# Identity products on TensorE ahead of the first transposes, and one value unit moved ahead of the first local softmax

## The reference

```python
x = x + local_attention(layernorm(x))              # 8 heads, chunks of 12 queries over 24 keys,
                                                   # relative positions, tanh cap 50, softmax, Wpost
x = x + cross_attention(layernorm(x), ctx_1024)    # 16 heads of 64, 512 context rows, rope on keys,
                                                   # clipped logits, softmax, Wo
x = x + mixture_ffn(layernorm(x))                  # 12 experts, top 3 routing, 128 -> 512 -> 128
```

## Time and profile before

| | us |
|---|---|
| median of 3 executions | 435.93 (434.12 to 436.87) |
| profiled execution, its time | 436.18 |
| profiled execution, its span | 434.5 |
| TensorE busy | 408.5 (94%) |
| VectorE busy | 333.3 (77%) |
| ScalarE busy | 176.6 (41%) |
| GpSimd busy | 258.9 (60%) |

### The profile page before, as it was taken

The page is one execution under the profiler, slowest core; times in us unless marked ns, Lnnn a source line. Parts: engine busy times, 40 slices in busy tenths (PEclk is TensorE's granted clock), DMA queues, the critical chain, the costliest instruction groups (busy, mean ns, idle before and its releaser), DMA issues.

```text
span 434.5 us, 8253 instructions
## 1 busy us (share of the span) xinstructions
PE 408.5 (94%) x3040; PEld 296.2 (68%) x3040; DVE 333.3 (77%) x657; ACT 176.6 (41%) x280; POOL 258.9 (60%) x225
## 2 busy tenths in 40 slices
PE   3979698999999999999998999999999999999996
PEld 2666576666666666666665666678767888888885
DVE  8989847998989976997768699787687881755444
ACT  6646434652644344452535353434447533000000
POOL 6814447898888978898879687778425750000000
PEclk9989979999999999999999999999999999999999
DMA  7678421131111111011110224536428740000000
GB/s 183 166 193 112 80 75 49 26 97 43 33 48 32 43 44 32 25 50 44 33 48 24 50 54 71 171 56 149 70 82 175 151 74 2 7 6 14 6 6 12
DMA packets 84745, 28.61 MB, mean 66 GB/s; under 512 B 71957, under 2 KB 79050, under 8 KB 84706
## 3 DMA queue, kind: packets, MB, share of 16 engines
q1 hardware_dynamic: 81556, 26.53, 27.5%
q10 hardware_dynamic: 3150, 1.56, 1.5%
HBM read 17.67 MB, written 2.02 MB: 45 GB/s over the span
## 4 chain that ended last, share of the span: by engine, by line
PE 66%; DVE 20%; issue 4%; ACT 4%; SPq 2%; POOL 2%; ACTq 1%; DMA 1%; DVEq 0%; POOLq 0%
PE psum L1204 9%; PE psum L1187 8%; PE psum L1387 5%; PE psum L1388 5%; PE psum L1386 5%; PE psum L1347 4%; PE psum L1349 4%; PE psum L1348 4%; PE psum L1223 3%; DVE rden L1615 3%; PE psum L1214 2%; DVE e_sb L1608 2%; PE psum L1006 2%; ACT e_sb L820 2%; PE psum L995 2%
## 5 line engine op out<-in xcount | busy, mean ns | idle before, releaser
L571 POOL TENSOR_TENSOR e_part<-e_sb 128x512 f32<-128x512 f32 x64 | 90.9, 1439 | 24.4 <-DVE e_sb L1608 21.2
L820 ACT ACTIVATE e_sb<-psum 128x1024 f32<-128x1024 f32 x64 | 62.2, 1021 | 99.0 <-PE psum L1187 99.0
L1187 PE MATMUL psum<-q_t,kT 64*128 64x256 f32 x512 | 64.2, 390 | 0.0
L1204 PE MATMUL psum<-e_sb,v_sb 128*64 128x256 f32 x512 | 63.9, 387 | 0.0
L1815 DVE SCALAR_TENSOR_TENSOR x_sb<-psum,dw,x_sb 128x128 f32<-128x128 f32 x96 | 33.7, 351 | 37.4 <-PE psum L1388 34.8
L1187 PEld LDWEIGHTS psum<-q_t,kT 64*128 64x128 f32 x512 | 46.8, 187 | 15.0 <-issue 9.3
L1615 DVE RECIPROCAL rden<-psum 128x256 f32<-128x256 f32 x32 | 55.8, 1745 | 0.1
L1608 DVE TENSOR_SCALAR e_sb<-e_sb 128x1024 f32<-128x1024 f32 x64 | 53.9, 880 | 1.1 <-ACT e_sb L820 1.0
L1204 PEld LDWEIGHTS psum<-e_sb,v_sb 128*64 128x64 f32 x512 | 33.8, 136 | 22.2 <-issue 6.5
L600 POOL TENSOR_TENSOR xeT_lo<-xeT,xeT_hi 128x512 fp32r<-128x512 f32 x24 | 31.3, 1307 | 28.4 <-ACT xeT_hi L834 28.2
L563 POOL TENSOR_TENSOR kT<-kT,raw 128x512 f32<-128x512 f32 x32 | 41.8, 1307 | 6.2 <-DMA raw<-rope_b 6.2
(11 more groups left out here) (202 smaller groups left out, 756.8 us busy)
## 6 DMA issues: line engine op xcount, KB each, us to landing
raw<-rope_b SPq DMA_DIRECT2D x112, 64.0 KB, 2.0
w_raw<-in_L_ffn_W_dram SPq DMA_DIRECT2D x96, 64.0 KB, 2.3
gates<-gate_dram SPq DMA_DIRECT2D x6, 768.0 KB, 4.8
ctx_sb<-in_ctx_dram SPq DMA_DIRECT2D x4, 256.0 KB, 6.2
vbd<-v_dram SPq DMA_DIRECT2D x16, 52.6 KB
v_dram<-v_tok SPq DMA_DIRECT2D x4, 136.0 KB
raw<-in_L_xattn_Wkv_dram SPq DMA_DIRECT2D x2, 256.0 KB, 5.2
kT<-in_L_xattn_Wkv_dram SPq DMA_DIRECT2D x2, 256.0 KB, 5.3
```

Of the source, the lines that this page charges most:

```text
L571: pool.tensor_tensor(e_part[:, p % 2, half, :, :], e_sb[:, i % ERING, :, 0, :], e_sb[:, i % ERING, :, 1, :], ALU.add)\
L820: act.activation(e_sb[:, i % ERING, :, :, :].rearrange("p a k t -> p (a k t)"), psum[:, a:a + 2, :].rearrange("p a b -> p (a b)"), ACT.Exp ...
L1187: mm = pe.matmul(psum[:, 2 * (i % 2) + a, t * S:(t + 1) * S], key_slot(p)[rows, kt * P:(kt + 1) * P], q_t[rows, j % 2, p % 2, :], start=Tr ...
L1204: mm = pe.matmul(psum[DX * a:DX * a + DX, pv_bank(p), 0:S], v_sb[g % 2][:, kt, 2 * pp + a, :], e_sb[:, i % ERING, a, t, :], start=(kt == 0 ...
```

## The change

It has two parts. On TensorE it adds `keep_busy(n)`, n products of the identity with itself into a part of PSUM bank 4 that is written over later: 11 between the moment `ident` is made and the wait for the weights, 8 after the position table is turned, and one ahead of each of the token tiles 1 to 7. Each is a full fp32 product of 128 x 128 with 128 columns; nobody reads the result. The second part moves one step each on two engines: on ScalarE the read of unit 5 goes ahead of `local_softmax(0)`, and on TensorE unit 7 goes ahead of `turn_weights_local(0)`.

```diff
@@ scalar
             value_unit(4)
             shift_positions(act, 1, 2)
+            value_unit(5)
             local_softmax(0)
-            value_unit(5)
             shift_positions(act, 1, 3)
@@ tensor
+            def keep_busy(n):
+
+                for _ in range(n):
+                    pe.matmul(psum[:, 4, 0:P], ident[:, :], ident[:, :], start=True, stop=True)
+
             pe.wait_ge(s["chain_pool"], 2)
+            keep_busy(11)
             pe.wait_ge(s["ld_aw"], 80)
...
             pe.transpose(psum[:, 1, P:P + NPOS], pos_sb[:, :], ident[0:NPOS, 0:NPOS]).then_inc(s["awT_ps"], 1)
+            keep_busy(8)
             for i in range(NT):
+                if i:
+                    keep_busy(1)
                 pe.wait_ge(s["xn_done"], i + 1)
...
             local_logits(5)
+            unit(7)
             turn_weights_local(0)
-            unit(7)
             unit(8)
```

## The result

The changed kernel took 437.9 us (median of 22 executions, 434.49 to 439.68) where the kernel before took 435.92 (22 executions, 432.51 to 438.13). The ratio of the two is put at 1.0037 with an interval of 1.002 to 1.0054, which is +1.6 us, or 0.9 to 2.4 (the medians themselves differ by 2.0). The median of 437.9 is inside the range of 434.0 to 438.1, near its upper end, and within 1% of the time before, but the rise is more than the forecast +0.3. The profiled execution took 438.42 us with a span of 436.7, 2.2 us more than before.

What follows compares the result with a forecast made beforehand. TensorE was taken to bound most of the span, but VectorE the chain from 10.9 to 24.9 us. +0.7 (a) - 0.4 (b) + 0 (moved unit) = +0.3 us, from 435.93 to 436.2 us; range 434.0 to 438.1.

Steps and rivals of the forecast that it cites:

- (a): TensorE at 24.94 us: longer wait for the context, clock already low on resuming; +0.7 us, bounds +0.8 and -1.4.
- (b): SyncE's queue: stores start 0.4 to 1.2 us sooner, so the bias load clears ScalarE's issue near 50 us; -0.4 us.
- the moved unit: Unit 5's read ahead of chunk 0's Tanh on ScalarE, unit 7 ahead of its turn on TensorE; 0, bounds ±0.3 us.
- The cover of GpSimd's clearing: VectorE's first sine table multiplication, started late, still ends at 18.54 behind GpSimd's clearing of vbd; 0, bounds 0 and 0.6 us.
- The start on TensorE: Up to the context: last token tile turned near 12.4 to 12.9 us, against 10.9; TensorE idle at 20.4 to 21.3.
- a sign of being wrong: The prediction counts as wrong if, among other signs, ScalarE's eight issues change by more than 0.7 us in sum.
- the read fits in there: Unit 5's read of 0.60 us fits ScalarE's 0.70 us of idleness ahead of the Tanh at 37.97, by less than 0.1.
- The slower rival: Identity products don't lift the clock before the token tiles and delay the start: +2.2 us, 438.1, up to +4; chance 0.17.
- The faster rival: Identity products and earlier work keep TensorE's clock high through 24.9 to 31 us: together -2.0 us, 433.9; chance 0.18.

Runs made afterwards that it cites:

- the last run: Kernel before with ScalarE's DMA issues split, 11 identity products ahead of the context's turns and 6 more ahead of the second projection: 434.22 us, ratio 0.995.
- the run with the filled wait: Changed kernel with 20 more identity products in TensorE's wait for the context: 435.55 us, ratio 0.9987 against the kernel before.
- the first wait filled: Kernel before with 11 identity products in TensorE's wait for the context (21.6 to 24.9 us); alone: 435.03 us, ratio 0.9976.
- the second filled alone: Kernel before with 12 identity products in TensorE's wait near 52 us, ahead of the second projection: 435.46 us, ratio 0.9987.
- both waits filled: Kernel before with 11 identity products in TensorE's wait for the context and 12 in its wait near 52 us: 435.36 us, ratio 0.998.
- the split: Kernel before with ScalarE reading chunk 2's turned outputs between its two groups of four DMA issues, not behind all eight: 434.75 us, ratio 0.9967.

## Why the prediction held, and where it was off

The measured +1.6 us lies in the range, but the range held it by its width. Of the three terms of +0.3, the +0.7 of (a) came in size and not by its path, the -0.4 of (b) didn't come, and the 0 of the moved unit was too low. The cover of GpSimd's clearing, at 0, was right.

*The cover of GpSimd's clearing.* Right. The first multiplication of the sine table started at times from 14.15 us (the changed kernel) to 15.35 (the last run) and ended at 18.54 to 18.57 in each of the twelve traces whose chain shows it; the second ended at 20.0. Most of these starts lie ahead of the clearing of vbd at 14.78, the one before's of 14.39 too. They lie under the clearing of bd, which the prediction left out and which stands right in front of it (kernel before):

```profile
12.98 1.86 POOL L545 MEMSET bd<- 128x2112 f32 x1
14.78 3.50 POOL L546 MEMSET vbd<- 96x4080 f32 x1
```

VectorE waited through both. That is the lock that "SBUF — State Buffer" of the Trainium skill describes in "SBUF: two separate sides", and the traces agree with it: an op that starts under one of the two clearings ends behind the second. The late start itself was tested by luck, in the run with the filled wait: relM began at 12.47 us in place of 11.78, and the first multiplication ended at 18.57 all the same.

*The start on TensorE.* The direction was right, the sizes were too large for this trace. The last token turn ended at 11.3, where the text had 12.4 to 12.9: the eight products began at 6.81 and not at 7.7, since I took the end of the position turn from the slow trace, and a pair of product and turn took 0.33 and not 0.42 us. (In rows of many, a product took 0.24 us at 2.4 GHz and 0.41 at 1.2, where I had 0.26 and 0.5.) TensorE was thus idle from 19.3 and not from 20.4 to 21.3, and relM was not late at all (11.79 against 11.78). But the run with the filled wait, the same kernel up to there, has the forecast's sizes: its eleven products took 5.06 us in place of 4.14, the weights' turns started at 6.43 and took 1.06, and the last token turn ended at 12.29. How soon the clock rises at the start differs from one execution to the next, and the forecast had one case of it.

*(a) The clock at 24.94.* The fall was forecast rightly: 0.50 already in the context's turns, 1.11 us for them. The step behind it failed, that the clock comes back at the same moment as before and +0.7 us stays on TensorE's chain. The clock came back sooner, by 28.6 us, and TensorE was at its first unit at 30.32 us against 30.36, so that on its own path the term was 0. That a cost near the +0.7 was measured all the same (the products alone +1.1 us, by an interval of 0.2 to 2.1, and the fill of the wait took 2.2 us from the changed kernel) is in part luck, for it came by another path. The relative products, slow at the low clock, release ScalarE's position stores, and these became the chain: they began 0.85 us later, and then their trip was longer. From the end of their last issue to the first shift it took 35.47 - 31.34 = 4.1 us in the changed kernel and 3.9 with the products alone, against 33.69 - 30.63 = 3.1 before and 3.0 with the wait filled. (The bound of -1.4 calls 4.8 us work at 0.50, of which the first 0.8 still ran at 1.00; the difference that it takes holds.)

The clock's part doesn't rest on single traces alone. Each execution has a mean granted clock on record, taken over all of it, the low stretch behind the second projection included. It was 0.992 or more in 58 of the 99 executions of the kernel before that stand beside the experiments, in 1 of 22 of the changed kernel, in none of 12 with the products alone, in 20 of 36 with only moved steps (three kernels), in 56 of 60 with the first wait filled (five kernels), and in 12 of 12 with the second filled alone. Within the kernel before, the 58 had a median of 435.7 us, and the 31 at 0.988 or below one of 437.2.

*(b) SyncE's queue.* Wrong. SyncE did start its stores 2.4 us sooner, at 17.87, but four issues took 4.85 in place of 3.23 us, and the 24 spreads 21.23 in place of 19.38, so the bias load issued at 51.86 and not before 50. ScalarE's eight issues took 6.71 and not 5.6; that is 0.68 more than before, just short of the 0.7 that the text had set as a sign of being wrong. The -0.4 didn't arrive: the failed step is that a sooner start of SyncE's list is a sooner end. Whether its end and the length of ScalarE's issues hang together is open. Over the unsplit kernels the eight were shortest (5.61 us) where the bias load ended first (50.35, ScalarE's step alone) and longest (7.83 us) where it ended last (53.06, both waits filled), but between these two there is no order, and no run moved that load alone.

*The moved unit.* The forecast of 0 with bounds of 0.3 was too low, as far as the traces tell: the read takes its 0.5 us ahead of the Tanh in the changed kernel and in both runs of its own that move it, and moves it by 0.25 to 0.5 us. In the changed kernel the Tanh came 1.6 us behind the start of VectorE's first sum, where the text had 0.6. The failed step is "the read fits in there". It took the end of the shift's issue from one trace (37.41), and that end lay at 37.67, 38.01 and 38.46 in these three. By time, 1.0013 and 1.0014 are not certain, but with the 1.0026 of the products they make 1.0039 or 1.0040, beside the measured 1.0037.

The slower rival (products that don't lift the clock) was wrong in its mechanism: at 4.14 us for eleven they lift it inside the first eleven, and in the run in which they took 5.06 the eight products behind the position turn were fast (2.05 us). The faster rival's place was right and its trigger wrong: what keeps the clock high at 24.9 is work in the wait itself. That was worth 1.0 us against the kernel before, where the rival had -1.4 for it.

Open is why the stores' trip was 1 us longer in the two traces with products at the start and a low clock, and 2.7 to 3.5 us in all the others, those with a low clock and no such products among them. The filled wait brought it back to 3.0 us, but no run changed that trip alone, so how a microsecond of this pair of traces gets from TensorE's clock into the trip is not shown.

## What to carry to other kernels

Warming TensorE up before its first work pays only if the work that it speeds up is on the chain; if another engine sets the next meeting point, the time gained turns into a longer wait, and the clock can be lost at just that point. Put the filler products into the last wait ahead of the work that counts, check which bank they write, and let them end before the work comes: six of them at 0.41 us each stood in its way in the last run. When a step is put into another engine's idle time, take the idle time from more than one trace: here it was 0.1 us longer than the step in one, and too short in three.

## What the runs showed of the hardware that was not expected

The granted clock of one place differs between kernels that are the same up to it. Of the profiled kernels without products ahead of the context, two had it low only from about 26.5 us (before, and the split), three had it low already in the context's turns, wholly or in part (0.93 to 1.12 us for them: the moved steps, ScalarE's step, the second fill), and one never had it low there:

```profile
24.90:31.40 6.50, 6.42 (x187) 1.00 0.75 181
```

(TensorE's step alone.) With a fill it was 1.00 in all five such kernels. There is an order in it. TensorE's wait for the context was 3.09 us where the clock never fell, 3.32 and 3.34 where it fell at about 26.5, 3.94 where it fell inside the context's turns, 4.06 and 4.25 where it was low from their start, and 5.64 in the two kernels with products at the start, where it fell near 22. In the six without products the queries and keys took 6.33, 6.07, 6.05, 5.46, 5.32 and 5.11 us in the same order, that is, the clock had risen the sooner at the start. Whether the length of the wait decides, or wait and fall both follow from that rise, no run separates. So one trace doesn't tell what the kernel before loses there; the mean gain of 1.0 us does.

A DMA issue takes 0.6 us in one trace and up to 2.2 us in another, for the same transfer in the same place (the second of ScalarE's eight: 0.61 with its step alone, 2.18 with both steps; SyncE's bias load: 0.53 and 1.52). The eight of ScalarE took from 5.61 to 7.83 us over the unsplit kernels, and in the kernel before and the changed one they stand on the chain.
